# An encoder kernel in which the inverse softmax sums are transposed by transfers through memory instead of by TensorE

## What is computed

```
for l in range(L):                                     # L = 4
    y = _layer_norm(h, ln_a[l, 0], ln_b[l, 0])
    q, k, v = ...                                      # y @ attn_w[l, :3] + attn_b[l, :3], 16 heads
    scores = jnp.einsum('bhqd,bhkd->bhqk', q, k) * inv_sqrt_dk
    p = jax.nn.softmax(scores, axis=-1)
    o = jnp.einsum('bhqk,bhkd->bhqd', p, v).transpose(0, 2, 1, 3).reshape(b, s, D)
    h = h + o @ attn_w[l, 3] + attn_b[l, 3]
    y = _layer_norm(h, ln_a[l, 1], ln_b[l, 1])
    h = h + jax.nn.relu(y @ w1[l] + b1[l]) @ w2[l] + b2[l]
```

## Time and profile before

| | us |
|---|---|
| median of 3 runs (2016.5 to 2016.9) | 2016.61 |
| the profiled execution | 2017.28 |
| span of its profile | 2015.5 |
| the 32 jobs, by the first and the last turning of `rb` | 48.3 to 1218.0 |

### The profile page before, as it was taken

One profiled execution on the slowest core, in us unless ns is written; L12 is line 12 of the kernel. 1 busy time (PEld: TensorE's weight loads), 2 busy tenths in 40 slices (PEclk: granted clock), 3 DMA queues, 4 the chain that ended last, 5 costly groups with the idle time before them and its releaser, 6 DMA issues. The chain is left out here.

```text
span 2015.5 us, 42310 instructions
## 1 busy us (share of the span) xinstructions
PE 1992.8 (99%) x16486; PEld 1662.6 (82%) x16486; DVE 1297.4 (64%) x3340; ACT 1034.2 (51%) x3520; POOL 216.2 (11%) x257
## 2 busy tenths in 40 slices
PE   8999999999999999999999999999999999999999
PEld 5888888888888888888888887788888888877776
DVE  6767767767767767767768764767776646323232
ACT  5665666666666666666665662555455521111111
POOL 1101000000000000000000000000000000334444
PEclk9999999999999999999999999999999999999999
DMA  3100000200000400000000001300000100035542
GB/s 94 57 32 12 1 2 2 72 2 2 1 2 2 163 2 2 1 2 2 1 1 2 2 2 40 150 1 1 1 1 1 64 1 16 27 93 158 169 136 67
DMA packets 27203, 69.84 MB, mean 35 GB/s; under 512 B 9920, under 2 KB 17825, under 8 KB 23680
## 3 DMA queue, kind: packets, MB, share of 16 engines
q1 hardware_dynamic: 18432, 59.42, 8.7%
q0 software_dynamic: 6400, 5.63, 1.1%
q10 hardware_dynamic: 2176, 2.10, 0.3%
HBM read 61.16 MB, written 17.40 MB: 39 GB/s over the span
## 5 line engine op out<-in xcount | busy, mean ns | idle before, releaser
L595 ACT ACTIVATE probs<-bank,nmax 128x256 f32<-128x256 f32 x1024 | 471.2, 480 | 233.6 <-DVE nmax L796 233.1
L796 DVE TENSOR_REDUCE nmax<-bank 128x2 f32<-128x512 f32 x512 | 321.9, 681 | 48.8 <-PE bank L421 48.7
L434 PE MATMUL bank<-ident,probs 128*128 128x128 f32 x2048 | 272.9, 276 | 1.7 <-DVE pts L804 1.1
L434 PEld LDWEIGHTS bank<-ident,probs 128*128 128x128 f32 x2048 | 229.2, 140 | 50.0 <-issue 33.7
L466 PE MATMUL bank<-yT,weights 128*128 128x256 f32 x1024 | 236.7, 379 | 0.0
L604 ACT ACTIVATE pts<-bank 128x512 f32<-128x512 f32 x256 | 157.0, 613 | 153.7 <-PE bank L434 152.6
L478 PE MATMUL bank<-weights,aT 128*128 128x256 f32 x1024 | 231.7, 379 | 2.2 <-ACT probs L595 1.9
L595 ACT ACTIVATION_READ_ACCUMULATOR probs<-bank,nmax 128x1 f32 x1024 | 216.6, 212 | 0.0
L478 PEld LDWEIGHTS bank<-weights,aT 128*128 128x128 f32 x1024 | 191.9, 190 | 28.0 <-issue 2.8
L804 DVE COPY pts<-bank 128x512 f32<-128x512 f32 x256 | 175.5, 685 | 46.6 <-PE bank L434 42.3
L466 PEld LDWEIGHTS bank<-yT,weights 128*128 128x128 f32 x1024 | 187.3, 190 | 21.6
(11 more groups left out here) (233 smaller groups left out, 2970.6 us busy)
## 6 DMA issues: line engine op xcount, KB each, us to landing
wqkv<-in_experts SPq DMA_DIRECT2D x16, 1024.0 KB, 5.1
weights<-in_wtok SPq DMA_DIRECT2D x4, 2048.0 KB, 10.4
wqkv<-in_experts SPq DMA_DIRECT2D x16, 512.0 KB, 3.7
expert_rows<-xT_all SPq DMA_DIRECT2D x10, 546.0 KB, 16.6
xrows<-expert_rows SPq DMA_DIRECT2D x16, 273.0 KB, 3.2
weights<-in_wtok SPq DMA_DIRECT2D x3, 1024.0 KB, 4.7
wqkv<-in_wqkv SPq DMA_DIRECT2D x1, 3072.0 KB, 17.6
weights<-in_shared SPq DMA_DIRECT2D x1, 3072.0 KB, 12.5
```

The lines of the kernel that those rows point to most:

```text
L434: last = pe.transpose(g[:, (NT * x + kb) * P:(NT * x + kb + 1) * P], p[:, x, kb * P:(kb + 1) * P], ident[:])
L595: last = nc.scalar.activation(probs[u % 8][:, x, :], g[:, x * S:(x + 1) * S], ACT.Exp, bias=nmax[j % 2][:, col:col + 1], accum_out=rsum[j ...
L796: nc.vector.tensor_reduce(nmax[j % 2][:, col:col + 2], g[:].rearrange("p (x s) -> p x s", x=2), AX.X, ALU.max, negate=True).then_inc(s_max, 1)
```

## The change

- VectorE's `recips` is replaced by `inverse(j, qt)`, a reciprocal of 16 columns, twice a job, with no spreading to `rb`. `inverse(j, 0)` stands in pass (j, 1) behind `o_norm(j-1)` and waits until ScalarE has taken all exponentials of groups 0 and 1. `inverse(j, 1)` stands in pass (j, 3), behind the last `copy_pt`, and waits for those of groups 2 and 3.
- SP's `inverse_T(j, qt)` stores the 128x16 tile `rinv` to a buffer in memory (`inverses`) in the order half, head, token, so that the tokens of one head are neighbours: 2048 single elements of 4 bytes. It waits for that store, then loads the buffer with two transfers into `rT`, one for each half of the features, in which every head's 128 numbers (512 bytes) are read to 16 partitions.
- TensorE's `r_T`, ScalarE's `r_out` and the unit `rT` in bank 7 are gone.
- `o_norm(j-1)` moves behind the fourth `row_max` and the first `copy_pt` of pass (j, 1), and waits for the loads of both `qt`.
- `rT` and `rinv` have two buffers. The loads of weights on SP stand between the inverses: layer l's behind `inverse_T` of job 2, 9 or 17 with qt = 0, and the six loads of the next stage behind layer 3's.

```diff
-                    use((j, "v"), 7), use((j - 2, "down", 0), 0), use((j - 1, "rT"), 7)
+                    use((j, "v"), 7), use((j - 2, "down", 0), 0)
...
+            def inverse_T(j, qt):
+                n = NT * j + qt
+                sp.wait_ge(s_inv, n + 1)
+                if j:
+                    sp.wait_ge(s_rT[qt], 16 * KD * j)
+                sp.dma_start(inverses[n % 2].rearrange("k h x q -> q (k h x)"), rinv[n % 2][:], allow_slow_non_contiguous=True).then_inc(s_turned, 16)
+                if j >= 2:
+                    evacuated(sp, (j - 2, "o"))
+                sp.wait_ge(s_turned, 16 * (n + 1))
+                for k in range(KD):
+                    sp.dma_start(rT[j % 2][:, k, qt * P:(qt + 1) * P],
+                                 inverses[n % 2, k].to_broadcast((H // KD, DK, P))).then_inc(s_rT[qt], 16)
+
+            for j in range(JOBS):
+                for qt in range(NT):
+                    inverse_T(j, qt)
+                    for l in range(1, L):
+                        if (j, qt) == (max((l - 1) * B - 1, 0) + 2, 0):
+                            layer(l)
...
-            def r_T(j):
-                if real(j):
-                    transposed((j, "rT"), rb[:].rearrange("p i n d -> p i (n d)"), s_rb, j + 1)
...
-            def r_out(j):
...
-                release(nc.scalar.activation(rT[:], g[:], ACT.Copy), (j, "rT"))
...
-            def recips(j):
...
-                step.up(nc.vector.reciprocal(rinv[:], rsum[j % 2][:]))
...
+            def inverse(j, qt):
+                if not real(j):
+                    return
+                n = NT * j + qt
+                for u in range(8 * qt, 8 * qt + 8):
+                    evacuated(dve, (j, "S", u))
+                if n >= 2:
+                    dve.wait_ge(s_turned, 16 * (n - 1))
+                nc.vector.reciprocal(rinv[n % 2][:], rsum[j % 2][:, qt * H:(qt + 1) * H]).then_inc(s_inv, 1)
...
             def o_norm(j):
                 if not real(j):
                     return
-                evacuated(dve, (j, "rT"))
+                for qt in range(NT):
+                    dve.wait_ge(s_rT[qt], 16 * KD * (j + 1))
...
-                    if c == 0:
-                        recips(j - 1)
                     row_max(j, c, 0)
                     row_max(j, c, 1)
-                    if c == 1:
-                        o_norm(j - 1)
...
                     if c == 1:
+                        o_norm(j - 1)
+                        inverse(j, 0)
                         fed_forward(j - 2, 1)
                         attended(j - 1)
...
                     if c == 3:
+                        inverse(j, 1)
                         relu(j - 1, 3)
```

38 lines of the change are left out of this document (15 added, 23 removed).

## The result

The changed kernel takes 2021.8 us (median of 10 runs, 2018.8 to 2023.9), the kernel before, on the same chip between them, 2016.9 us (median of 10, from 2016.5). The ratio is 1.0023, with an interval from 1.0015 to 1.0031: slower by 0.2%, where 14 us less were forecast.

The account below looks back on a forecast made before the run. TensorE, busy 99% and nearly without waits in the encoder, was taken as the bound. Minus 16.4 for slots, plus 1.5 and 1 once-only, gave minus 14: 2002.6 us, forecast 1999 to 2006, range reaching to 2010.

Parts of the forecast that it names:

- Bank 0: Scores of group 1 start 0.53 us earlier and need this bank freed by VectorE; 0.25 us left, cost 0.
- the new wait on VectorE: `inverse(j, 0)` waits for group 1's last exponential, inside an idle of 1.90 us; cost 0.
- the later product: `oT` on VectorE behind four row maxima and a copy, ready with 1.3 us to spare; cost 0 per job.
- the chain: Store, wait and two loads turning the inverses through memory: 10.9 us, between 3.9 and 15.8, against 15.7 of room; cost 0.
- The rival of the slot given back on VectorE: Bank 0 or the wait for exponentials returns 0.1 to 0.4 us of each 0.53: 2006 to 2012.6 us; chance 0.14.
- The first rival: Slow 4-byte store stalls TensorE in every job, slower than before, for instance 2140 us; chance 0.13.
- The slot, 31 x 0.53: Four transposes of `rb` removed from TensorE in each of 31 jobs, 0.53 us each: 16.4 us gained.
- The store, 7.3 us: SP's store of 2048 pieces: 1.7 us plus 128 x 0.044 for pieces per DMA engine; dearer reading 12.2 us.
- The once-only costs: Late first product, 1.5 us, and waits for turned inverses around job 17, 1 us; job 0's own counted as enough.
- the late product: In pass (1, 1), without `ffn_down` ahead, the product ends 1.8 us late, less some 0.6 of idle; counted 1.5.
- the chains: Job 0: room 11.4 us, enough for 10.9, up to 4.4 short; job 17: up to 7 us once, counted 1.
- The slot in front of the first scores: TensorE waits for exponentials right behind the first of 32 slots, so removing it gives nothing.

Follow-up runs that it names:

- b_wide: Changed kernel with the store's same 8 KB written as 128 pieces of 64 bytes, token by token, so the turning is left out: 2002.2 us, ratio 0.9923.
- d_none: Changed kernel without store, loads or the wait for them; `rT` holds ones, so the division by the sums is left out: 2002.2 us, ratio 0.9923.
- l_dve: Changed kernel, complete, with VectorE turning the inverses in 32 x 32 blocks before a store of 128-byte pieces: 2002.5 us, ratio 0.9927.
- q_pad8: Changed kernel, complete, tokens packed, heads 4096 bytes apart in the buffer instead of 512: 3207.9 us.
- p_heads: Changed kernel with tokens packed but heads stored 64 KB apart; loads read a buffer filled once, so no turning: 2539.9 us, one run.
- c_half: Changed kernel storing only 8 of 16 heads (1024 pieces) and loading these twice: 2026.0 us, one run.
- o_best: `l_dve` with the product `o_norm` back in its old place, behind the second row maximum: 2002.6 us, ratio 0.9928.
- a_again: The changed kernel, unaltered, run again in the first group: 2032.2 us, ratio 1.0076.
- g_both: Changed kernel, slow store kept, with the next stage's six loads spread over jobs 18 to 20 and job 0's inverses turned on TensorE: 2003.9 us, ratio 0.9939.
- a_third: The changed kernel, unaltered, run again in the fourth group: 2020.5 and 2019.6 us, only two usable executions.
- q_pad9: Changed kernel, complete, tokens packed, heads 4608 bytes apart in the buffer instead of 512: 2085.8 us, ratio 1.0341.
- f_first: Changed kernel with job 0's inverses turned on TensorE as before and job 0's product in its old place: 2025.3 us, ratio 1.0035.

## Why the prediction was wrong

**What held.** TensorE sets the pace, and the slots taken out of it are worth their time: `b_wide`, `d_none` and `l_dve` are 14.4 to 16.0 us under the kernel before of their own group, where the sum said 14. Part of the agreement is luck, as the terms below show. Bank 0, the new wait on VectorE and the later product cost nothing per job. No job in the steady part waits for the chain, as forecast: 10.2 + 4 us fit into the room that I had counted at 15.7. The rival of the slot given back on VectorE falls with the steady distance: at most 0.09 us of the 0.53 is missing, and the next paragraph finds it on TensorE. The first rival, stalls in every job, falls for this kernel, although `q_pad8` and `p_heads` show what it looks like.

**The slot, 31 x 0.53.** Mis-sized. It is 37.71 - 37.27 = 0.44 us a job. In the earlier trace rows the transposes end with scores beginning 0.53 us behind their start; after the change the eight transposes of `turn_probs` take 651.18 - 650.22 = 0.96 us up to the scores, where they took 0.88 up to `rb`. The change of form from transposes to scores costs 0.08 us wherever it stands, and I had counted it as removed. 31 x 0.44 = 13.6 instead of 16.4. That `b_wide` is nevertheless 14.9 us shorter in its span comes from places that I did not have: jobs 1, 4, 28 and 29 gained 1.1, 0.7, 1.2 and 1.2 us, and 1.6 us behind the encoder are the luck of the executions that were profiled.

**The store, 7.3 us.** Mis-sized: 10.1 to 11.1 us by SP's waits. It lay between my bounds (1.7 and 12.2), but I had picked the value by a price per piece, which `c_half` refutes. Ends of a range say nothing of the law between them: the price of a 1 KB packet in the earlier trace rows was of another kind.

**The once-only costs are the step that failed.** I counted 2.5 us, 1.5 for the late product and 1 for the chains. Against `b_wide` the slow store costs 17.2 us, all but the 1.8 in job 4 through late chains. The 1.5 came out by luck: counted from the scores of pass (1, 0), `b_wide` has its first product 2.1 us later than the kernel before, and gets 0.7 back in job 1 beyond the slot. But the late product itself costs some 0.1 us (`o_best` against `l_dve`), and 1.3 us are the two gaps in `pv`. (The slot in front of the first scores, which I had rightly taken as worth nothing, gives nothing.) With the measured terms, -13.6 for the slots, -1.7 more in jobs 4, 28 and 29, +1.4 at the start, +17.2 for the slow store, the last product comes 3.3 us later than before. Four things went wrong in it:

- *Their size hung on the store's and I took the cheap end in both.* My text has the room of job 0's chain at 11.4 us, "enough for 10.9, up to 4.4 us short", and for job 17 "up to 7 us, once; with a store of 4 us it would be 0. I count 1". With 10.7 us of store and 3.8 from the issue of the loads to the start of the product on VectorE, 14.5 in all, job 0 was short by some 3 us, and the first product is 3.0 us later than in `b_wide`; in job 17 the wait was 7.76. Both numbers were in the text, and the sum left them out. The forecast's own store of 7.3 us would already have ended behind 690 + 7.3 us, with its loads needed at 694: 1 us was never a middle value.
- *A stall was counted once, but it is paid twice.* Behind each, the granted clock of TensorE fell to the lower level, and eight matmuls took 3.6 instead of 1.9 us. In job 0 that is 1.7 us more, paid in the distance of job 1. In job 17 the distance grew by 45.2 - 37.3 + 39.0 - 37.3 = 9.6 us for a wait of 7.76. No wait in the encoder of before, at most 1.2 us, came with it, but the trace of before had such a stretch elsewhere (1255 to 1265 us).
- *The last job is a place of its own.* It has less work between its store and its product. The forecast has no term for it; it cost 1.1 us, and 2.5 in `a_again`.
- *Gaps of TensorE for which the trace names no releaser.* In front of `pv` they add up to 0.6 us with a store of 1.3 and with none, 0 to 5.6 us with a store of 10 to 11 us (none in `g_both`, 0.8 in `a_third`, 5.6 in `c_half`), and 35.9, 169.1 and 396.6 us in `q_pad9`, `p_heads` and `q_pad8`. In the changed kernel the one in job 4 costs 1.8 us. So a slow store makes them longer, but some are there without it. A late fetch of TensorE's instructions would look like this, and the list of DMA queues has two with instructions:

```profile
q8 instruction: 133, 2.18, 0.5%
q14 instruction: 66, 0.53, 0.1%
```

That the gaps are such fetches is argued, not shown. `g_both` lacks them with a slow store, and `f_first`, in which TensorE has the same program, has them in pass (1, 1); their cause stays open.

**The chances.** Slower had 0.13, all of it on a mechanism that pays in every job. What happened is a third way, with its price in my own text (4.4 + 7 us): a rival made of once-only stalls at the dear end of the store, 2002.6 + 4.4 + 6 us, at about 2013 us without what came on top. It was neither weighed nor in the range, which ended at 2010.

## What to carry to other kernels

When one unknown duration sits in several terms of a sum, carry each of its ends through all of them together, and make the case of the dear end a rival of its own: here the same store decided the chains of job 0 and job 17, set at 1 us together, and that of the last job, which the sum did not have. To turn a small tile through memory, let an engine make the pieces contiguous first: a 0.21 us transpose in 32 x 32 blocks on VectorE took the store from 10 us to 1.5, and with it the stalls; that kernel (`l_dve`) runs in 2002.5 us, 0.9927 of the kernel before. Where the slow store must stay, look for the first job and for bulk loads in front of it in the queue: covering these two alone gave 2003.9 us.

## What the runs showed of the hardware

- A store of 2048 pieces of 4 bytes to memory, by SP's mean wait: 9.9 to 11.1 us with tokens packed and heads 512 bytes apart; 10.3 with half the pieces; 11.8, 31.5 and 20.7 us with the heads 4608 bytes, 4096 bytes and 64 KB apart; 5.4 and 3.8 us with the tokens 16 and 64 bytes apart. The same bytes as 128 pieces of 64 bytes take 1.3 us, and a load in 2048 pieces of 4 bytes 2.6 us.
- At equal distance between the heads the two buffers took different times: 10.4 and 14.0 us at 4608 bytes, 41.4 and 24.0 at 4096, each store in its own half of the job.
- After a wait of TensorE of 2.9 or 7.8 us the clock granted to it was 0.57 and 0.63 over the next 4 us, and eight matmuls took 3.6 us instead of 1.9.
- The slowest stores come with long gaps in TensorE's row that have no releaser, up to 22.3 us for one in `q_pad8`, though TensorE takes nothing from that store. Two gaps of 0.3 us are there without any store, and make 64 matmuls last 3.2 us instead of 1.9.
- The unaltered changed kernel had medians of 2021.8 and 2032.2 us and two runs near 2020 us in three groups, while the medians of the kernel before stayed within 2015.8 to 2018.2. From the issue of the store to that of the loads the medians were 10.3, 11.3 and 10.3 us: one microsecond more of each store came with 10 us more in all, at the few places where the chain exceeds its room.
